# A mixture's down matrices as float16 pairs, and squares 512 columns at a time

## The reference

```python
x = layernorm(x + linear_attention(x))        # 4 heads, chunks of 64, gates of rank 16; o * rsqrt(mean(o*o)) over 128, silu gate, Wo
x = layernorm(x + mixture_0(x))               # the mixture that is changed
x = layernorm(x + differential_attention(x))
x = layernorm(x + mixture_1(x))

# mixture_0: 8 experts, the 2 with the largest router probability for each token, and a shared expert
normed = layernorm(x) * ln_gamma + ln_beta
comb = two gates for each token
for e in range(8):
    g, u = split(normed @ gate_up_w[e].T)     # 256 -> 2 x 768
    out += comb[:, e] * ((silu(g) * u) @ down_w[e].T)    # 768 -> 256
```

## Time and profile before

| | |
|---|---|
| median of 3 runs | 2595.52 us (2593.21 to 2602.96) |
| the profiled execution | 2593.12 us, of it the span 2591.4 us |
| granted TensorE clock, mean | 0.945 |
| PE, DVE, ACT, POOL busy | 2310.2, 1588.0, 1356.6, 687.3 us |
| linear attention, mixture's first part, tile loop | 0 to 444, 444 to 564.4, 564.4 to 1095.3 us |

### The profile page before, as it was taken

How to read it: one execution, slowest core, us unless ns; L and a number is a source line. 1 busy time by engine, 2 the same in 40 slices (tenths; PEclk the granted TensorE clock), 3 DMA queues, 4 the chain that set the end, 5 groups by cost and what they waited for, 6 DMA issues and landing times.

```text
span 2591.4 us, 49152 instructions
## 1 busy us (share of the span) xinstructions
PE 2310.2 (89%) x17112; PEld 1390.9 (54%) x17112; DVE 1588.0 (61%) x2623; ACT 1356.6 (52%) x2587; POOL 687.3 (27%) x754
## 2 busy tenths in 40 slices
PE   7999995979999999867769998899999998997998
PEld 5777774546666666656613333433343333336887
DVE  3566565633333333379887777777777777714887
ACT  6766662213433332223218888788778876883000
POOL 1222122003333333336632223222322232221000
PEclk9999997989999999979859999999999999988999
DMA  4233223662222222234310100010001100001000
GB/s 160 82 106 121 93 74 113 235 192 35 52 36 38 38 38 36 34 132 154 131 68 25 49 27 26 26 45 26 29 24 45 35 28 16 26 2 66 17 25 25
DMA packets 89607, 164.01 MB, mean 63 GB/s; under 512 B 15920, under 2 KB 63536, under 8 KB 87712
## 3 DMA queue, kind: packets, MB, share of 16 engines
q1 hardware_dynamic: 75744, 142.10, 15.8%
q0 software_dynamic: 13632, 18.77, 4.5%
HBM read 99.81 MB, written 60.49 MB: 62 GB/s over the span
## 4 chain that ended last, share of the span: by engine, by line
PE 59%; DVE 7%; ACT 6%; issue 5%; DMA 2%; SPq 1%; POOL 0%; ACTq 0%; DVEq 0%; POOLq 0%
PE PS L2020 10%; PE PS L1283 7%; PE PS L58 6%; PE PS L60 6%; PE PS L59 6%; PE PS L2069 6%; PE PS L2041 5%; ACT E L1838 4%; PE PS L2036 3%; DVE NM L1937 2%; PE PS L1270 2%; PE PS L1972 2%; DVE TT L1475 2%; PE PS L1995 1%; PE PS L1196 1%
## 5 line engine op out<-in xcount | busy, mean ns | idle before, releaser
L1838 ACT ACTIVATE E<-PS,SCL 128x512 f32<-128x512 f32 (+2 forms) x1280 | 733.8, 650 | 186.2 <-PE PS L2069 182.9
L1937 DVE TENSOR_REDUCE NM<-PS 128x2 f32<-128x1024 f32 (+3 forms) x608 | 692.1, 1163 | 220.8 <-PE PS L2041 211.1
L2020 PE MATMUL PS<-E,VP 128*32 128x256 f32 (+1 forms) x5120 | 380.1, 380 | 0.6 <-ACT OT L1866 0.6
L1771 POOL TENSOR_SCALAR_AFFINE_SELECT E<-E 128x512 f32<-128x512 f32 x256 | 162.9, 636 | 496.2 <-ACT E L1838 496.2
L1102 DVE SCALAR_TENSOR_TENSOR XIL<-PS,XSC,XIH 128x128 f16<-128x128 f32 x142 | 43.3, 346 | 342.5 <-ACT XIH L896 342.5
L2069 PE MATMUL PS<-QK 50*128 50x512 f16 (+3 forms) x1152 | 224.6, 334 | 28.1 <-ACT E L1838 27.5
L931 ACT ACTIVATE HB<-PS 128x768 f32<-128x768 f32 x71 | 57.6, 811 | 300.8 <-PE PS L1270 300.8
L2020 PEld LDWEIGHTS PS<-E,VP 128*32 128x32 f32 x5120 | 110.0, 110 | 165.2 <-issue 127.9
L1283 PE MATMUL PS<-WALL,HB 128*128 x852 | 195.7, 379 | 1.0 <-ACT HB L931 1.0
L846 POOL DMA_INDIRECT XB<-x_normed,IDX x71 | 71.0, 1000 | 432.4 <-DVE GAT L1118 310.9
L2041 PE MATMUL PS<-QK 48*128 48x512 f16 (+3 forms) x1152 | 182.3, 349 | 3.7 <-DVE NM L1937 3.7
(11 more groups left out here) (337 smaller groups left out, 4165.3 us busy)
## 6 DMA issues: line engine op xcount, KB each, us to landing
parts<-PP SPq DMA_DIRECT2D x32, 512.0 KB, 3.0
WIN<-in_we SPq DMA_DIRECT2D x16, 768.0 KB, 5.1
QK<-parts SPq DMA_DIRECT2D x96, 128.0 KB
WALL<-pairs_of_weights SPq DMA_DIRECT2D x7, 1536.0 KB
pairs_of_weights<-WPH SPq DMA_DIRECT2D x16, 384.0 KB, 2.3
pairs_of_weights<-WPL SPq DMA_DIRECT2D x16, 384.0 KB, 3.2
QK<-parts SPq DMA_DIRECT2D x96, 64.0 KB
WALL<-in_we SPq DMA_DIRECT2D x7, 768.0 KB
```

The source lines that it names most:

```text
L1771: e.affine_select(out=E[:, m % NE, :, 0:128], in_=E[:, m % NE, :, 0:128], pattern=[[0, 4], [1, 128]], compare_op=ALU.is_ge, fill=0.0, base ...
L1838: e.activation(dst, src, ACT.Exp, scale=K.SCL[:]).then_inc(S.ex, 1)
L1937: e.tensor_reduce(dst, src, AX, ALU.max).then_inc(S.mx, 1)
L2020: a = e.matmul(PS[32 * jj:32 * jj + 32, 7, 512 - n + c0:512 - n + c1], VP[b % 2][:, kt, 17 * hd:17 * hd + 32], E[:, m % NE, jj, c0:c1], st ...
```

## The change

It makes the down matrices pairs too, so that a third piece for each expert passes through `WIN`, `WPH` and `WPL`. There are 24 pieces instead of 16, three a step: `high(3t)` stands behind the table load and ahead of the `GA` work, `low(3t)` behind `GG`. The scratch in memory holds 9216 float16 columns for each expert and is loaded in one transfer, as many bytes as before. In the tile loop the hidden values are scaled by one over the largest of their row (a reduction, a floor and a reciprocal on VectorE, then a scaled copy on ScalarE), turned, and split into high and low parts in two pieces of 512 and 256 columns; the down product is then 18 float16 products of 256 columns. The Silu waits for `up0` alone and stands ahead of the split on ScalarE; the turning of the next inputs stands ahead of `up`. `scales()` builds three scales instead of two, and the gate is multiplied by the row's largest. In linear attention the squares are four instructions of 512 columns on ScalarE with two buffers, and VectorE sums them behind `low`.

```diff
@@ gla, SyncE
-            e.dma_start(WIN[:], A["we"][c // 2][:, 1536 * (c % 2):1536 * (c % 2) + 1536]).then_inc(S.g_ws, 16)
+            e.dma_start(WIN[:], A["we"][c // 3][:, 1536 * (c % 3):1536 * (c % 3) + 1536]).then_inc(S.g_ws, 16)
...
             if t < 8:
-                pairs(2 * t)
-                weights(2 * t + 1)
+                for c in (3 * t, 3 * t + 1):
+                    pairs(c)
+                    weights(c + 1)
@@ gla, ScalarE
                 explog()
+                high(3 * t)
                 for p in HALF:
                     kb, c = bank[5 + p], slice(512 * p, 512 * p + 512)
...
-                high(2 * t)
+                high(3 * t + 1)
...
-                high(2 * t + 1)
+                high(3 * t + 2)
...
                 for i, b in enumerate((0, 2, 1, 3)):
-                    for hd in QUAD:
...
-                        n = own.act.on(e.activation(SQ[:], PS[:, bank[(3, 4, 7, 0)[b]], 128 * hd:128 * hd + 128], ACT.Square, accum_out=SS[:, 4 * b + hd:4 * b + hd + 1]))
-                e.wait_ge(own.act.sem, n)
+                    e.wait_ge(S.pe_o, 8 * t + 4 + i + 1)
+                    if 4 * t + i > 1:
+                        e.wait_ge(S.sm, 4 * t + i - 1)
+                    e.activation(SQ[i % 2][:], PS[:, bank[(3, 4, 7, 0)[b]], :], ACT.Square).then_inc(S.sq, 1)
+                e.wait_ge(S.sm, 4 * t + 4)
@@ gla, VectorE
+                low(3 * t)
                 for h in HALF:
                     e.wait_ge(S.ep, 2 * t + h + 1)
...
-                low(2 * t + 1)
+                low(3 * t + 2)
+                for i, b in enumerate((0, 2, 1, 3)):
+                    e.wait_ge(S.sq, 4 * t + i + 1)
...
+                    e.tensor_reduce(SS[:, 4 * b:4 * b + 4], SQ[i % 2][:].rearrange("p (h v) -> p h v", h=4), AX, ALU.add).then_inc(S.sm, 1)
@@ moe, ScalarE, turn s
+            if s < NT:
+                gu = PS[:, 3 * (s % 2):3 * (s % 2) + 3, :].rearrange("p k s -> p (k s)")
+                e.wait_ge(S.pe_up0, s + 1)
+                if s > 0:
+                    e.wait_ge(S.hh, s)
+                e.activation(SI[:], gu[:, 0:768], ACT.Silu, scale=UN[:, 0:1]).then_inc(S.si, 1)
             if s > 0:
...
-                e.activation(HB[:, 768:1536], PS[:, b0:b0 + 2, :].rearrange("p k s -> p (k s)")[:, 0:768], ACT.Copy).then_inc(S.ht, 1)
+                for c0, c1 in split:
+                    e.activation(HTH[:, c0:c1], turned_up[:, c0:c1], ACT.Copy, scale=XSC[:, 2, s - 1:s]).then_inc(S.ht, 1)
             if s + 1 < NT:
                 high(s + 1)
             if s < NT:
...
+                e.wait_ge(S.rr, s + 1)
+                e.activation(HI, HI, ACT.Copy, scale=RR[:, s % 2:s % 2 + 1]).then_inc(S.hs, 1)
@@ moe, VectorE, scales()
-            for k in HALF:
+            for k in (0, 1, 2):
                 v.tt(CT, TE[:].unsqueeze(2).to_broadcast([128, 72, 8]), CNT[:, 233:241].unsqueeze(1).to_broadcast([128, 72, 8]), ALU.is_equal)
@@ moe, VectorE, turn s
+                for i, (c0, c1) in enumerate(split):
+                    e.wait_ge(S.ht, 2 * s - 1 + i)
+                    e.scalar_tensor_tensor(out=HTL[:, c0:c1], in0=turned_up[:, c0:c1], scalar=XSC[:, 2, s - 1:s], in1=HTH[:, c0:c1],
+                                           op0=ALU.mult, op1=ALU.subtract).then_inc(S.htl, 1)
...
+                v.n = own.dve.on(e.tensor_reduce(RM[:, s % 2:s % 2 + 1], HI, AX, ALU.max, apply_absolute_value=True))
+                v.wait()
+                v.put(e.tensor_scalar(RM[:, s % 2:s % 2 + 1], RM[:, s % 2:s % 2 + 1], 1e-30, None, ALU.max))
...
+                e.reciprocal(RR[:, s % 2:s % 2 + 1], RM[:, s % 2:s % 2 + 1]).then_inc(S.rr, 1)
@@ moe, TensorE, turn s
-                r = e.value_load(TI[0:1, s:s + 1], min_val=0, max_val=7 * 4608)
-                r16 = e.value_load(TI[0:1, 72 + s:73 + s], min_val=0, max_val=7 * 9216)
+                r16 = e.value_load(TI[0:1, s:s + 1], min_val=0, max_val=7 * 9216)
...
-                e.wait_ge(S.hh, s)
+                e.wait_ge(S.hs, s)
...
+            if s + 1 < NT:
+                turn_rows(s + 1)
             if s < NT:
...
                 up_rows(PS[:, b0 + 2, :], s, r16, 2).then_inc(S.pe_up, 1)
-            if s + 1 < NT:
-                turn_rows(s + 1)
...
-                e.wait_ge(S.ht, s)
                 for i in range(6):
-                    a = e.matmul(PS[:, b1 + 2, 0:256], HT[:, i, :], wide(r_last, 3072 + 256 * i, 256), start=i == 0, stop=i == 5)
+                    e.wait_ge(S.htl, 2 * s - 1 + i // 4)
+                    b = slice(128 * i, 128 * i + 128)
+                    a = mm3(e, PS[:, b1 + 2, 0:256], HTH[:, b], HTL[:, b], high(r_last, 6144 + 256 * i, 256), high(r_last, 7680 + 256 * i, 256), i == 0, i == 5)
```

More of the change, by code:

```diff
@@ L127, in gla @@
     ST8 = sb("S", [128, 2, 2, 4, 128])
-    SQ = sb("SQ", [128, 128])
+    SQ = [sb(f"SQ{i}", [128, 512]) for i in range(2)]
     WIN, WPH, WPL = sb("WIN", [128, 1536]), sb("WPH", [128, 1536], F16), sb("WPL", [128, 1536], F16)
@@ L170, in sp @@
             if t > 0:
-                pairs(2 * t - 1)
+                pairs(3 * t - 1)
                 if t < 8:
-                    weights(2 * t)
+                    weights(3 * t)
             if t < 6:
@@ L390, in dve @@
             if t < 8:
-                low(2 * t)
+                low(3 * t + 1)
             if t > 0:
@@ L796, in sp @@
                 e.wait_ge(S.m_st0, nth(6))
-                second(7, 3584, 4608)
+                expert(7, 7168, 9216)
                 e.wait_ge(S.pe_sdn, 16)
-                pairs(7, 4096, 6144)
-                second(7, 3072, 3584)
+                expert(7, 4096, 7168)
             e.wait_ge(S.sxa, 2 * t + 2)
@@ L971, in dve @@
         e.wait_ge(S.qs, 1)
-        e.tensor_reduce(QNS[:, 2:3], PS[:, 7, 0:16], AX, ALU.add).then_inc(S.qs, 1)
+        sums = PS[:, 7, 0:24].rearrange("p (x k) -> p x k", k=3)
+        e.tensor_reduce(QNS[:, 3:4], sums[:, :, 2], AX, ALU.add).then_inc(S.qs, 1)
+        e.wait_ge(S.qs, 2)
+        e.tensor_reduce(QNS[:, 2:3], sums[:, :, 0:2], mybir.AxisListType.XY, ALU.add).then_inc(S.qs, 1)
         hidden(0)
@@ L1117, in gate @@
                 e.wait_ge(S.yo, s - 1)
-            e.tensor_reduce(GAT[:, s % 2:s % 2 + 1], G2[:], AX, ALU.add).then_inc(S.gat, 1)
+            v.n = own.dve.on(e.tensor_reduce(GAT[:, s % 2:s % 2 + 1], G2[:], AX, ALU.add))
+            v.wait()
+            e.scalar_tensor_tensor(out=GAT[:, s % 2:s % 2 + 1], in0=GAT[:, s % 2:s % 2 + 1], scalar=UN[:, 1:2], in1=RM[:, s % 2:s % 2 + 1],
+                                   op0=ALU.mult, op1=ALU.mult).then_inc(S.gat, 1)
         def prepare(s):
@@ L1216, in pe @@
         e.wait_ge(S.m_one, 1)
-        e.matmul(PS[:, 7, 0:16], ONE[:], K.WSS[:], start=True, stop=True).then_inc(S.pe_ss, 1)
+        e.matmul(PS[:, 7, 0:24], ONE[:], K.WSS[:], start=True, stop=True).then_inc(S.pe_ss, 1)
         turn(0)
@@ L2351, in program @@
         small.update(LGA=sb("LGA", [128, 32, 8], F32, first), X=None, QK=None, MRF=None, IDB=None, MR=None,
-                     WSS=sb("WSS", [128, 16], F32, first), WSC=sb("WSC", [128, 16], F32, first), GBN=sb("GBN", [128, 2], F32, first),
-                     banks=[[ctx.enter_context(nc.semaphore(f"s{i}_{j}")) for j in range(n)] for i, n in enumerate((62, 63, 22))],
+                     WSS=sb("WSS", [128, 24], F32, first), WSC=sb("WSC", [128, 24], F32, first), GBN=sb("GBN", [128, 2], F32, first),
+                     banks=[[ctx.enter_context(nc.semaphore(f"s{i}_{j}")) for j in range(n)] for i, n in enumerate((64, 64, 19))],
                      left=ctx.enter_context(nc.semaphore("left")), cleared=ctx.enter_context(nc.semaphore("cleared")),
@@ L2358, in program @@
         D = dict(XN=dram("x_normed", (4224, 260)), XR=dram("x_resid", (4224, 256)),
-                 PARTS=dram("parts", (2, 4, 2, 4, 128, 1024), F16), VP=dram("values", (4, 128, 8, 288)), WP=dram("pairs_of_weights", (8, 128, 6144), F16))
+                 PARTS=dram("parts", (2, 4, 2, 4, 128, 1024), F16), VP=dram("values", (4, 128, 8, 288)), WP=dram("pairs_of_weights", (8, 128, 9216), F16))
         D = namedtuple("Dram", D)(**D)
```

95 lines of the change are left out of this document (49 added, 46 removed).

## The result

The changed kernel takes 2636.01 us, the median of four runs (2634.41 to 2637.37); the kernel before, run beside it, 2599.24 (2593.21 to 2603.78). The ratio is 1.0143, with a 95% interval of 1.0117 to 1.0169: slower by 1.4%. The profiled execution took 2636.11 us, its span 2634.3, which is 42.9 more than before. I cut both spans at the same three places: the start of VectorE's copy of the last logits (L444 before, L449 after), of the first `up0` of the tile loop, and of VectorE's last output rows.

The account below looks back on a forecast made before the run. TensorE was taken to bound the tile loop before, a chain with the sequencer after: 2593.1 + 6 + 2 + 10 + 3 + 0.3 + 3.6 = 2618, median 2.4 higher, 2620 us. Range 2598 to 2642; forecast's own 2606 to 2635.

Parts of the forecast that it names:

- What bounds the loop: Tile loop: TensorE's work sets the 7.35 us turn before; afterwards Silu, high part, low part and PE's sequencer do.
- 7.44: Tile loop: forecast length of a turn in us, 0.09 above 7.35, so +6 us over 70 turns.
- 2.37: Tile loop: us from low part to next `up0`, for 12 register instructions, one address load, wait and hand-over.
- Rule against row: Tile loop: skill's queue of 64 lets the sequencer finish early; trace rows show a register instruction held until the copy ends.
- a free sequencer: Tile loop, rival: the sequencer is not in the way, a turn of 7.15, 2600 us; chance 0.16.
- The other chain: Tile loop: path through the row's largest, about 5 us against 5.6 of TensorE's products and waits, hidden by some 0.6.
- The last turn: End of the tile loop: the scaling is exposed, 13.7 instead of 11.8 us, +2.
- Linear attention: `high(3t)` waits for its load and delays `GA`, costing 1.1 to 1.7 us a step, +10; step 0 and squares extra.
- Step 0's +3: Linear attention, step 0: a load with the longest landing (7.3) and an uncovered `high` cost +3 us.
- a gain is excluded: Linear attention, squares: no gain, as `low` ends after ScalarE's squares could; +0.3 us at the end.
- The way in: Before the tile loop: a third round of scales costs 2.4 us and small instructions 1.2, +3.6, all on the path.
- the worse cases: Rival: the turn reaches 7.7 as both chains meet, or a longer stall lowers the clock; 2620 + 18 and more, chance 0.10.

Follow-up runs that it names:

- silulate: The changed kernel with the Silu behind the high parts on ScalarE instead of ahead of them; 2617.68 us, a turn of 7.48.
- bankfirst: The changed kernel with the next address loaded ahead of the down product and the second bank's 256 columns split and multiplied first; 2588.86 us, a turn of 6.90.
- early: The changed kernel with the next tile's address loaded ahead of the down product instead of behind it; 2611.27 us, a turn of 7.25.
- fixed: The changed kernel with the down product's matrices at a constant place, without register addresses (results wrong for most tiles); 2610.27 us, a turn of 7.16.
- turn: The changed kernel with the early address load, the second bank's columns first and the Silu behind the high parts; 2579.83 us, a turn of 6.79.
- lowfirst: The changed kernel with the third piece's low part ahead of the two copies of turned output in linear attention; 2625.90 us.
- best: The changed kernel with the edits of early, bankfirst and lowfirst, and the making of the scales spread over VectorE's idle times; 2568.61 us.
- final: The kernel best with the Silu behind the high parts as well; 2559.61 us, ratio 0.9844 to the kernel before.
- twice: The changed kernel with each tile's address loaded twice a turn, the second load's register feeding the down product; 2669.57 us, a turn of 8.27.

## Why the prediction was right, and where it was off

- **What bounds the loop.** Right: it goes from TensorE's pace to the chain of Silu, high part, low part and sequencer. silulate shortens the turn by the 0.14 that it takes out of the chain. bankfirst shortens it by 0.35, where its first product was to come 0.6 sooner; from 900 to 930 us its trace has no idle time of 60 ns or more between TensorE's products, where early's has 0.34 us a turn, so that what is left of the turn is mostly TensorE's own work.
- **The size of the turn**, "7.44", was 7.60 to 7.62, above the "7.4 to 7.5" that the prediction named as its sign of being right. This is the term that was mis-sized, +20 us in 70 turns instead of +6. The first parts held: 2.79 to the Silu was 2.80, 0.80 was 0.80, 0.69 was 0.69. The hand-over from ScalarE to VectorE was 0.09, not 0.04. The last part, "2.37" from the low part to `up0`, was 2.43 in the turn shown and 2.49 in the median. In the median turn it is 0.04 to the first register instruction, 1.58 for the twelve, 0.65 for the load, 0.11 for the wait and 0.10 to the product. So the load, the wait and the hand-over were priced rightly, and the twelve register instructions, taken at 0.124 each or 1.49, cost 0.09 more: in most turns one or two of them come later than 0.124 after the one before (1.52 in all in the turn shown, up to 1.70 in others). Why they do is open.
- **Rule against row.** The row decided rightly for this kernel, and the rule for the kernel without register instructions: fixed runs at 7.16, and the price that the prediction gave for a free sequencer was 7.15. But neither describes what the sequencer does there: it seems to stand at a wait in that kernel too, and has so little left to do behind it that it is done before the array. What decides in these kernels is the work that the sequencer has behind the wait, 1.58 us of register instructions.
- **The other chain**, hidden by "some 0.6": the scaled row was ready 0.8 ahead of TensorE's turning of it, and did not decide in the changed kernel. It had more room than I gave it later, as turn showed.
- **The last turn**: the forecast was +2. The loop lost 23.3 us; from the first `up0` to that of the last tile it lost 20.2, and so 3.1 behind it.
- **Linear attention**: +10.3 against 13.3. `GA` is 1.40 later a step, as forecast, and six steps lose 1.35 on average. In this step 1.29 of the 1.40 are the wait for the load; in the six steps `GA` is 1.36 later on average and ScalarE waits 0.99 to 1.65 for the load, 1.34 on average. lowfirst gets more than that back, because it moves the root too. Step 0's +3 was +4 (the first square at 53.22, not 49.36). The term that was wrong is the squares': "a gain is excluded" holds for the steps whose `low` ends late, but not for step 0, where 3 us are won.
- **The way in**: 3.6 forecast, 4.5 in the one profile; with 124.2 to 127.6 for the same code its size is uncertain by more than the difference. The middle instruction of a round took 0.94 to 0.96 us, not the 0.76 that it took before; three rounds make 0.6 of it. That it lay on the path is shown by best and final.
- **The sum** was 16 us short: 15 in the loop and 1 in the way in, less 3 too much in linear attention, plus about 5 that vary between executions of unchanged code, less the 2.4 by which the median was to lie above the profiled execution (it lies 0.1 below). The result is inside the stated range, but outside the forecast's own 2606 to 2635 by 1 us: the mechanism was right, and that the total stays inside owes something to the width left for the worse cases and to the terms of opposite sign.

## What to carry to other kernels

Where TensorE's operands take their addresses from a register, count its sequencer as an engine of its own: a wait stops it, the register instructions behind the wait then cost 0.12 to 0.13 us each (1.58 for twelve here), and a load of the next address belongs ahead of the waits of a turn's last product, not behind them. When a serial chain runs over three engines, cut its first piece small and give the large one the time under the small one's products. And before a step is put on an engine, ask when its input was sent for: here 1.3 us a step hung on a load that went out behind two copies, and lowfirst, which makes the copies later, loses nothing by it.

## What the runs showed of the hardware that I had not expected

- One load of an address, with its register instruction and its check, took 0.65 us of the sequencer (twice), as long as six down products of 256 columns at 0.109.
- A VectorE product of 576 elements whose second input is every third number of a small table took 0.94 to 0.96 us; the comparison of as many elements ahead of it took 0.76, and so did the same product in the kernel before, where the second input was every second number.
- Stages whose code was the same in every kernel differed by up to 12.7 us between profiles (1490.3 to 1503.0), more than several single edits here were worth. Only the turn, of which there are 70 in each trace, could be read to 0.02 us.
